# Second-layer attention: the order of scores, turns and weights between groups of steps

## The chip, the cores and the metric

The kernel runs on one core of a Trainium2 chip. The metric is the device time of one execution in microseconds (us). The kernel before took 2488.93 us in the median of three runs (2488.81 to 2493.3).

## The reference

The kernel computes a decoder of four layers on a batch of four rows of 512 tokens with 128 features, all in float32. Each layer has an attention, a cross attention and a feed-forward part. The change touches the attention of layer 2 alone (layers are counted from 0). It has 16 heads of 8 features and adds up three attentions with gates of their own per token:

```python
q = _rope(x @ Wq, HD); k = _rope(x @ Wk, HD); v = x @ Wv
sc = jnp.einsum('bhsd,bhnd->bhsn', q4, ck4) * SCALE    # 32 compressed blocks of 16 tokens
a_comp = _masked_softmax(sc, comp_mask[None, None])
ss = jnp.einsum('bhsd,bhmd->bhsm', q4, ks4) * SCALE    # 16 selected tokens
a_sel = _masked_softmax(ss, (causal_sel & valid[:, None, :])[:, None])
sw = jnp.einsum('bhsd,bhtd->bhst', q4, k4) * SCALE     # a causal window of 32 tokens
a_win = _masked_softmax(sw, wmask[None, None])
out = g[..., 0:1] * out_comp + g[..., 1:2] * out_sel + g[..., 2:3] * out_win
return out @ Wo + bo
```

A softmax over a fully masked row gives zeros.

## The kernel before

**Two lanes.** The batch is split over two lanes. Lane 0 takes rows 0 and 2, lane 1 first a short preparation and then rows 1 and 3; each stage is done for both rows of a lane before the next stage begins. A lane has its own four PSUM banks, scratch and semaphores. Both lanes share the engines. For each engine a unit gives a generator that yields between pieces. A planner (`plan`, L3051) runs all pieces with estimated costs before the kernel is built, starting at each point the piece that can begin first, and so fixes one order per engine for the whole kernel. On the chip each engine works through that order and waits on semaphores.

**Layer-2 attention** (`l2_attn`, from L1736). After a prelude (projections, rotary position, compressed keys and values, the selection of two blocks, gates) the 512 queries of a row are handled in J = 16 steps of 32 queries. For a step the 16 heads x 32 queries are four tiles of 128 rows, and each row has C = 112 keys: 64 of the window, 32 compressed, 16 selected. Four steps form a group (GR = 4, NG = 4 groups). A step j of group g passes through these stages:

- **spread** (GpSimd, L1953): the queries times the head mask into `qb`, two buffers. It waits until the scores of step j - 2 are in PSUM.
- **scores** (TensorE, L1855): four products with `kall` into bank 0 or 1, by turns. It waits for the mask of step j - 2 and for `qb`. In float32 a product is two passes, so a step shows as 8 records.
- **mask** (VectorE, L2079): scores plus mask, from PSUM into `sc`, which has two buffers of a whole group.
- **shift** (VectorE, L2029 to L2036), once for a group: the maximum of each 16 keys, of each of the three parts (three small steps L2031, three small steps L2034), and the subtraction over 128x1792.
- **exponential** (ScalarE, L1941), once for a group, over 128x1792.
- **weigh** (VectorE, L2042 to L2057), once for a group: the sums, their reciprocals times the gates, three copies into `wt7`.
- **product** (GpSimd, L1968), once for a group: exponentials times weights over 128x1792.
- **turn** (TensorE, L1864): four transposes of a step's probabilities into bank 2, which is the only one. It waits for the copy of step j - 1.
- **copy** (ScalarE, L1936): bank 2 into `pT`, two buffers.
- **values** (TensorE, L1875): four products with `vall` into bank 3. The first of a group waits until the group before has been picked.
- **pick** (VectorE, L2065 and L2069), once for a group: the own head's part of bank 3 is kept and summed into `oT`.

After the last group the output projection (L1890) and two additions (L2091, L2094) end the unit. The normalization of the lane's next unit is worked in at the end (`norm.means`, `norm.apply`, `norm.tensor`, `norm.scalar`, `norm.gpsimd`).

**Orders before.** TensorE runs a loop over i that issues turn(i - 5), scores(i), values(i - 6), so the turns of group g begin right ahead of the scores of the second step of group g + 1, and scores and turns alternate. VectorE issues mask(i), after each fourth mask the shift of that group, then the first mask of the next group, weigh, and three more masks; a pick stands after the second mask. ScalarE alternates copies and, at each fourth index, an exponential. GpSimd issues spread(i + 1) and, at each fourth i, the product of the group before.

## Time and profile before

| | |
|---|---|
| median of 3 runs | 2488.93 us (2488.81 to 2493.3) |
| the profiled execution | 2484.5 us |
| its span | 2482.7 us |
| TensorE granted clock, mean of the span | 0.824 of full speed |
| VectorE busy | 1649.3 us |
| TensorE busy | 1928.5 us |
| ScalarE busy | 1035.8 us |
| GpSimd busy | 592.6 us |

The profile comes from one execution, which has its own time beside the median. The span is what the profiler saw between the first and the last instruction. Busy times of TensorE hold waits inside its pipeline, and the ends of its products are modelled. The names of engines in the rows are PE (TensorE, with PEld for its weight loads), DVE (VectorE), ACT (ScalarE) and POOL (GpSimd); "idle before" is followed by what ended most of the idle time. The rows come from the page, from the table by stretches, from the groups by line and from the timeline, in which successive instructions of one line are merged (x3).

### The profile page before, as it was taken

How to read it: one execution, taken by the hardware profiler on the slowest of the kernel's cores; microseconds unless marked ns; L12 is line 12 of the kernel's file. 1: busy time of each engine (PE TensorE's matmuls, PEld its weight loads, DVE VectorE, ACT ScalarE, POOL GpSimd, SP SyncE). 2: the span in 40 equal slices, each digit the busy share in tenths (PEclk: the TensorE clock that was granted, in tenths of full speed). 3: DMA queues.
4: the chain of work that ended last, by engine and by line, in shares of the span. 5: the costliest groups of instructions: out<-in, count | busy, mean ns of one | idle time of the engine just before them, and what ended most of it. 6: DMA issues, size and time to landing. Idle time of an engine off the chain costs nothing. (4 is left out here: it accounts for less than half of the span.)

```text
span 2482.7 us, 31166 instructions
## 1 busy us (share of the span) xinstructions
PE 1928.5 (78%) x11373; PEld 1097.1 (44%) x11378; DVE 1649.3 (66%) x3698; ACT 1035.8 (42%) x1618; POOL 592.6 (24%) x520
## 2 busy tenths in 40 slices
PE   4788887888797777799998867669866665699972
PEld 2553544546363232367776655545532221234331
DVE  5665757575666454453637898994469988985566
ACT  1226555564644343343333223233245345425561
POOL 0003323242330010000001543530025634721000
PEclk8888998989897688799999778766667877879965
DMA  4002112030302000000000000000000000000000
GB/s 159 1 1 57 43 44 55 17 82 7 92 1 89 1 1 1 1 22 1 1 1 1 1 1 1 1 1 1 1 0 1 0 0 0 0 1 1 1 5 13
DMA packets 19224, 43.78 MB, mean 18 GB/s; under 512 B 5323, under 2 KB 7935, under 8 KB 18175
## 3 DMA queue, kind: packets, MB, share of 16 engines
q1 hardware_dynamic: 19071, 41.78, 6.0%
q8 instruction: 91, 1.49, 0.3%
q14 instruction: 62, 0.51, 0.1%
HBM read 16.59 MB, written 1.05 MB: 7 GB/s over the span
## 5 line engine op out<-in xcount | busy, mean ns | idle before, releaser
L2265 PE MATMUL lane_banks<-l_attn_lane_hc,base 128*128 128x512 f32 x256 | 176.6, 806 | 111.4 <-DVE l_attn_lane_hc L2418 111.1
L2343 POOL TENSOR_TENSOR l_attn_lane_u<-l_attn_lane_xp,l_attn_lane_bn 128x512 f32<-128x512 f32 x128 | 182.1, 1449 | 190.4 <-ACT l_attn_lane_bn L2318 190.4
L2409 DVE TENSOR_TENSOR_SCAN l_attn_lane_h<-l_attn_lane_da,l_attn_lane_u 128x512 f32<-128x512 f32 x128 | 187.7, 1501 | 5.4 <-ACT l_attn_lane_da L2326 3.2
L595 POOL TENSOR_SCALAR lane_next_rstd<-lane_next_mv 128x4 f32<-128x4 f32 x48 | 12.9, 270 | 729.0 <-DVE lane_next_mv L572 729.0
L1644 ACT ACTIVATE l_ffn_lane_hT<-lane_banks,weights 128x512 f32<-128x512 f32 x128 | 87.9, 688 | 144.5 <-PE lane_banks L1598 144.1
L1448 ACT ACTIVATE l_attn_lane_ex<-lane_banks 128x768 f32<-128x768 f32 (+3 forms) x128 | 87.0, 703 | 138.1 <-PE lane_banks L1406 137.9
L2265 PEld LDWEIGHTS lane_banks<-l_attn_lane_hc,base 128*128 128x128 f32 x256 | 58.2, 249 | 189.3 <-DVE l_attn_lane_hc L2418 146.8
L1690 DVE SCALAR_TENSOR_TENSOR l_ffn_lane_eo<-lane_banks,l_ffn_lane_sel,l_ffn_lane_eo 128x128 f32<-128x128 f32 x224 | 63.0, 344 | 97.2 <-PE lane_banks L1620 96.4
L1620 PEld LDWEIGHTS lane_banks<-weights,l_ffn_lane_hT 128*128 128x128 f32 x1024 | 119.8, 192 | 15.8 <-issue 12.2
L1620 PE MATMUL lane_banks<-weights,l_ffn_lane_hT 128*128 128x128 f32 x1024 | 122.6, 276 | 0.9 <-DVE l_ffn_lane_eo L1690 0.9
L2318 ACT ACTIVATE l_attn_lane_bn<-lane_banks 128x512 f32<-128x512 f32 x64 | 37.9, 594 | 195.9 <-PE lane_banks L2259 192.9
L1509 DVE TENSOR_REDUCE l_attn_lane_mx<-lane_banks 128x4 f32<-128x1024 f32 (+2 forms) x64 | 94.6, 1488 | 28.7 <-PE lane_banks L1387 28.6
L978 PE MATMUL lane_banks<-f_attn_lane_work,weights 128*128 128x512 f32 x128 | 81.0, 753 | 32.9 <-ACT f_attn_lane_work L1098 32.0
L1953 POOL TENSOR_TENSOR l_attn_lane_qb<-l_attn_lane_qT,base 128x512 f32<-128x512 f32 x64 | 85.4, 1344 | 88.2 <-PE lane_banks L1855 75.3
L1855 PE MATMUL lane_banks<-l_attn_lane_kall,l_attn_lane_qb 128*128 128x112 f32 x512 | 85.7, 325 | 25.3 <-DVE l_attn_lane_sc L2079 19.3
L1936 ACT ACTIVATE l_attn_lane_turns<-lane_banks 112x512 f32<-112x512 f32 x64 | 37.3, 593 | 136.5 <-PE lane_banks L1864 136.4
L1855 PEld LDWEIGHTS lane_banks<-l_attn_lane_kall,l_attn_lane_qb 128*128 128x128 f32 x512 | 79.7, 238 | 29.9 <-DVE l_attn_lane_sc L2079 22.7
L1136 POOL TENSOR_TENSOR f_attn_lane_work<-f_attn_lane_work,f_attn_lane_rden 128x512 f32<-128x512 f32 x64 | 67.1, 1051 | 104.2 <-DVE f_attn_lane_rden L1177 104.2
L2573 ACT ACTIVATE l_xattn_lane_ex<-lane_banks 77x1024 f32<-77x1024 f32 x64 | 64.9, 1020 | 63.7 <-PE lane_banks L2504 63.7
L582 DVE TENSOR_SCALAR lane_rows<-x,lane_next_mv,lane_next_rstd 128x128 f32<-128x128 f32 x192 | 66.3, 415 | 33.6 <-POOL lane_next_rstd L596 33.3
L2326 ACT ACTIVATE l_attn_lane_da<-l_attn_lane_dt,a 128x512 f32<-128x512 f32 x128 | 85.9, 714 | 2.2 <-DVE l_attn_lane_h L2409 1.8
L2418 DVE TENSOR_TENSOR l_attn_lane_hc<-l_attn_lane_h,lane_banks 128x512 f32<-128x512 f32 x128 | 80.9, 672 | 3.3 <-PE lane_banks L2267 3.1
(531 smaller groups left out, 4700.8 us busy)
## 6 DMA issues: line engine op xcount, KB each, us to landing
f_attn_lane_work<-f_attn_lane_work SPq DMA_DIRECT2D x256, 64.0 KB, 2.0
weights<-packed SPq DMA_DIRECT2D x1, 4564.5 KB, 19.8
f_attn_lane_vb<-f_attn_lane_va SPq DMA_DIRECT2D x8, 512.0 KB, 4.5
f_attn_lane_vb<-f_attn_lane_va SPq DMA_DIRECT2D x8, 384.0 KB, 5.8
weights<-packed SPq DMA_DIRECT2D x1, 2320.0 KB, 8.4
weights<-packed SPq DMA_DIRECT2D x1, 2091.0 KB, 13.6
out<-x SPq DMA_DIRECT2D x4, 256.0 KB, 2.2
weights<-packed SPq DMA_DIRECT2D x1, 897.0 KB, 9.5
```

What stands on the lines that cost most here:

```text
L978: pe.matmul(ps(2 + n % 2), w("pairones"), sq, start=True, stop=True).then_inc(*s.up("norms_in_psum"))
L1448: act.activation(ex[:, kt % 2, h:h + 2, 0:T - P * kt], banks(0, 2)[:, :, 0:T - P * kt], ACT.Exp, scale=scale)\
L1509: v.tensor_reduce(mx[:, j, t, :], banks(0, R)[:, :, 0:n], AX.X, ALU.max).then_inc(*s.up("row_max"))
L1620: last = pe.matmul(ps(2)[:, tile(t)], hT[:, n % 2, c, tile(t)], w("m1_w2", (2 * (e - 1) + c) * D, (2 * (e - 1) + c + 1) * D), start=(c == ...
L1644: act.activation(hT[:, n % 2, c, :], ps(c), ACT.Relu, bias=w("m1_b1", b, b + 1)).then_inc(*s.up("hidden_ready"))
L1855: last = pe.matmul(ps(j % 2)[:, g * C:(g + 1) * C], qb[:, j % 2, tile(g)], kall[:, j, :], start=True, stop=True)
L1953: g_.tensor_tensor(qb[:, j % 2, :].rearrange("p (h q) -> p h q", h=A2_H), bc(qT[:, 32 * j:32 * j + 32], A2_H), w("headmask").rearrange("p ...
L2265: pe.matmul(ps(2 + c), w("ident"), hc[:, c, :], start=(n == 1), stop=(n == NS)).then_inc(*s.up("state_added"))
L2326: act.activation(da[:, i % 3, :], dt[:, c, :], ACT.Exp, scale=net.a3[:, c, n:n + 1]).then_inc(*s.up("da_ready"))
L2343: g.tensor_tensor(u[:, i % 3, :], dtx[:, c, :], bn[:, n % 2, :], ALU.mult).then_inc(*s.up("u_ready"))
L2409: v.tensor_tensor_scan(h[:, c, :], da[:, i % 3, :], u[:, i % 3, :], 0.0, ALU.mult, ALU.add).then_inc(*s.up("scanned"))
L2418: v.tensor_tensor(hc[:, c, :], h[:, c, :], ps(1), ALU.mult).then_inc(*s.up("hc_ready"))
```

## The change

The order in which the four engines issue the parts of this attention is written anew. Within a group q, TensorE issues all four scores, then for the group before it turn, turn, values, turn, values, turn, values; the last values of a group come after the first scores of the group after next. VectorE issues four masks, weigh of the group before, pick of the group before that, and then the shift of the group just masked. ScalarE issues the exponential of group q between the second and third copy of group q - 1. GpSimd issues the four spreads of a group and then the product of the group before. What each part computes, its buffers and the semaphores it waits on stay as they were. The planner lays out both lanes anew from these orders.

```diff
--- before.py
+++ after.py
@@ -1876,13 +1876,19 @@
                                  start=True, stop=True)
             last.then_inc(*s.up("values_in_psum"))
 
-        for i in range(J + 6):
-            if 5 <= i < J + 5:
-                yield from turn(i - 5)
-            if i < J:
-                yield from scores(i)
-            if i >= 6:
-                yield from values(i - 6)
+
+        for q in range(NG + 1):
+            for j in range(GR * q, GR * q + GR):
+                if q < NG:
+                    yield from scores(j)
+                if q >= 2 and j == GR * q:
+                    yield from values(j - GR - 1)
+            if q >= 1:
+                for j in range(GR * (q - 1), GR * q):
+                    yield from turn(j)
+                    if j % GR:
+                        yield from values(j - 1)
+        yield from values(J - 1)
         yield from norm.tensor(pe, ps(1), norm.to_come)
         yield
         pe.wait_ge(*s.at("o_ready", NG))
@@ -1926,19 +1932,25 @@
             act.wait_ge(*s.at("vwin_in_psum", q + 1))
             act.activation(vall[0:64, GR * q:GR * q + GR, :], ps(1 + q % 2)[0:64, :].rearrange("p (j d) -> p j d", j=GR), ACT.Copy)\
                .then_inc(*s.up("vwin_ready"))
-        for i in range(J + 5):
-            if i >= 5:
-                j = i - 5
+
+        def copy_turned(j):
+            yield
+            act.wait_ge(*s.at("pT_in_psum", j + 1))
+            if j >= 2:
+                act.wait_ge(*s.at("values_in_psum", j - 1))
+            act.activation(pT[0:C, j % 2, :], ps(2)[0:C, :], ACT.Copy).then_inc(*s.up("pT_ready"))
+
+        for q in range(NG + 1):
+            if q >= 1:
+                for j in range(GR * (q - 1), GR * q - 2):
+                    yield from copy_turned(j)
+            if q < NG:
                 yield
-                act.wait_ge(*s.at("pT_in_psum", j + 1))
-                if j >= 2:
-                    act.wait_ge(*s.at("values_in_psum", j - 1))
-                act.activation(pT[0:C, j % 2, :], ps(2)[0:C, :], ACT.Copy).then_inc(*s.up("pT_ready"))
-            if i % GR == GR - 1 and i < J:
-                g = i // GR
-                yield
-                act.wait_ge(*s.at("shifted", g + 1))
-                act.activation(sc[:, g % 2, :, :, :], sc[:, g % 2, :, :, :], ACT.Exp, scale=scale).then_inc(*s.up("exp_ready"))
+                act.wait_ge(*s.at("shifted", q + 1))
+                act.activation(sc[:, q % 2, :, :, :], sc[:, q % 2, :, :, :], ACT.Exp, scale=scale).then_inc(*s.up("exp_ready"))
+            if q >= 1:
+                for j in range(GR * q - 2, GR * q):
+                    yield from copy_turned(j)
         yield from norm.scalar(act, ps(1), norm.to_come)
 
     def gpsimd(g_):
@@ -1955,14 +1967,14 @@
 
         yield
         g_.wait_ge(*s.at("q_ready", 1))
-        yield from spread(0)
-        for i in range(J + 1):
-            if i + 1 < J:
-                yield from spread(i + 1)
-            if i >= GR and i % GR == 0:
-                g = i // GR - 1
-                if i == J:
-                    yield from norm.gpsimd(g_)
+        for q in range(NG + 1):
+            for j in range(GR * q, GR * q + GR):
+                if q < NG:
+                    yield from spread(j)
+            if q == NG:
+                yield from norm.gpsimd(g_)
+            if q >= 1:
+                g = q - 1
                 yield
                 g_.wait_ge(*s.at("weights_ready", g + 1))
                 g_.tensor_tensor(sevenths(g), sevenths(g), bci(wt7[:, g % 2, :, :].rearrange("p r n -> p (r n)"), 16), ALU.mult)\
@@ -2069,25 +2081,24 @@
             v.tensor_reduce(oT[:, P * g:P * (g + 1)].rearrange("p (j q) -> p j q", j=GR),
                             r[:, g % 2, :, :].rearrange("p j (h q) -> p j q h", h=4), AX.X, ALU.add).then_inc(*s.up("o_ready"))
 
-        for i in range(J + 6):
-            if i < J:
-                g = i // GR
+        for g in range(NG):
+            for j in range(GR * g, GR * g + GR):
                 yield
-                v.wait_ge(*s.at("scores_in_psum", i + 1))
-                if g >= 2 and i % GR == 0:
+                v.wait_ge(*s.at("scores_in_psum", j + 1))
+                if g >= 2 and j == GR * g:
                     v.wait_ge(*s.at("pT_in_psum", GR * (g - 1)))
-                v.tensor_tensor(sc[:, g % 2, i % GR, :, :], ps(i % 2)[:, 0:4 * C].rearrange("p (g c) -> p g c", g=4),
-                                bc(mask[:, i, :], 4), ALU.add).then_inc(*s.up("masked"))
-                if i % GR == GR - 1:
-                    yield from shift(g)
-            if i == J:
-                yield from norm.means(v, norm.to_come)
-            if i % GR == 0 and GR <= i <= J:
-                yield from weigh(i // GR - 1)
-            if i == J:
-                yield from norm.apply(v, norm.to_come)
-            if i >= 9 and i % GR == 1:
-                yield from pick(i // GR - 2)
+                v.tensor_tensor(sc[:, g % 2, j % GR, :, :], ps(j % 2)[:, 0:4 * C].rearrange("p (g c) -> p g c", g=4),
+                                bc(mask[:, j, :], 4), ALU.add).then_inc(*s.up("masked"))
+            if g >= 1:
+                yield from weigh(g - 1)
+            if g >= 2:
+                yield from pick(g - 2)
+            yield from shift(g)
+        yield from norm.means(v, norm.to_come)
+        yield from weigh(NG - 1)
+        yield from norm.apply(v, norm.to_come)
+        yield from pick(NG - 2)
+        yield from pick(NG - 1)
         st.link(v.tensor_tensor(x, x, bc(w("a2_bo"), NT), ALU.add))
         yield
         v.wait_ge(*s.at("y_in_psum", 1))
```

## Rows read from the trace of the kernel before

**Rows 1.** The page: the span, and busy time by engine (share of the span).

```profile
span 2482.7 us, 31166 instructions
PE 1928.5 (78%) x11373; PEld 1097.1 (44%) x11378; DVE 1649.3 (66%) x3698; ACT 1035.8 (42%) x1618; POOL 592.6 (24%) x520
```

**Rows 2.** Table by stretches: us, busy PE, PEld, DVE, ACT, POOL, clock, DMA, GB/s.

```profile
1360.00:1395.00 35.00, 28.92 (x168) 22.60 (x169) 27.51 (x61) 10.69 (x19) 11.58 (x8) 0.65 0.00 0
...
1410.00:1469.00 59.00, 37.59 (x288) 29.93 (x288) 56.70 (x117) 14.94 (x20) 29.86 (x18) 0.72 0.00 1
...
1325.00:1695.00 370.00, 267.51 (x1971) 207.47 (x1972) 318.50 (x728) 111.67 (x184) 149.74 (x102) 0.76 0.00 1
```

**Rows 3.** VectorE's groups by line and shape, 1325 to 1695: busy us, mean ns | idle.

```profile
L2079 DVE TENSOR_TENSOR l_attn_lane_sc<-lane_banks,l_attn_lane_mask 128x448 f32<-128x448 f32 x64 | 38.3, 618 | 14.3 <-PE lane_banks L1855 14.0
...
L2042 DVE TENSOR_REDUCE l_attn_lane_sm<-l_attn_lane_sc 128x112 f32<-128x1792 f32 x16 | 32.2, 2015 | 2.1 <-ACT l_attn_lane_sc L1941 1.6
...
L2034 DVE TENSOR_SCALAR l_attn_lane_mx<-l_attn_lane_mx 128x64 f32<-128x64 f32 x16 | 9.7, 609 | 0.5
...
L2034 DVE TENSOR_SCALAR l_attn_lane_mx<-l_attn_lane_mx 128x32 f32<-128x32 f32 x16 | 6.2, 387 | 0.0
...
L2034 DVE TENSOR_SCALAR l_attn_lane_mx<-l_attn_lane_mx 128x16 f32<-128x16 f32 x16 | 5.0, 311 | 0.0
```

**Rows 4.** Timeline 1325 to 1370: start, us, engine, line, operation [idle before].

```profile
1325.30 1.17 PE L1790 MATMUL lane_banks<-weights,lane_xnT 128*32 128x3 f32 x32 [0.44 <-DVE x L1728]
...
1357.96 2.01 DVE L2029 TENSOR_REDUCE l_attn_lane_mx<-l_attn_lane_sc 128x112 f32<-128x1792 f32 x1
...
1360.45 0.37 DVE L2034 TENSOR_SCALAR l_attn_lane_mx<-l_attn_lane_mx 128x64 f32<-128x64 f32 x3
...
1360.86 2.02 DVE L2036 TENSOR_TENSOR l_attn_lane_sc<-l_attn_lane_sc,l_attn_lane_mx 128x1792 f32<-128x1792 f32 x1
...
1362.91 1.70 ACT L1941 ACTIVATE l_attn_lane_sc<-l_attn_lane_sc 128x1792 f32<-128x1792 f32 x1 [2.87 <-DVE l_attn_lane_sc L2036]
...
1365.25 2.01 DVE L2042 TENSOR_REDUCE l_attn_lane_sm<-l_attn_lane_sc 128x112 f32<-128x1792 f32 x1
...
1369.20 0.35 DVE L2057 COPY l_attn_lane_wt<-l_attn_lane_sm 128x64 f32<-128x64 f32 x3
...
1369.63 3.24 POOL L1968 TENSOR_TENSOR l_attn_lane_sc<-l_attn_lane_sc,l_attn_lane_wt 128x1792 f32<-128x1792 f32 x1 [11.40 <-DVE l_attn_lane_wt L2057]
```

**Rows 5.** Timeline, single steps of the loop and the end of a row.

```profile
1347.49 1.94 PE L1855 MATMUL lane_banks<-l_attn_lane_kall,l_attn_lane_qb 128*128 128x112 f32 x16
...
1353.80 1.92 PE L1855 MATMUL lane_banks<-l_attn_lane_kall,l_attn_lane_qb 128*128 128x112 f32 x8 [1.43 <-POOL l_attn_lane_qb L1953]
...
1414.38 0.66 PE L1875 MATMUL lane_banks<-l_attn_lane_turns,l_attn_lane_vall 112*32 112x128 f32 x8
...
1414.97 0.81 PE L1864 MATMUL lane_banks<-base,l_attn_lane_sc 128*112 128x128 f32 x4
...
1460.07 3.24 POOL L1968 TENSOR_TENSOR l_attn_lane_sc<-l_attn_lane_sc,l_attn_lane_wt 128x1792 f32<-128x1792 f32 x1 [2.35 <-DVE l_attn_lane_wt L2057]
...
1464.50 0.60 ACT L1936 ACTIVATE l_attn_lane_turns<-lane_banks 112x512 f32<-112x512 f32 x1 [8.70 <-PE lane_banks L1864]
...
1475.11 0.68 DVE L2065 TENSOR_TENSOR l_attn_lane_tokens<-lane_banks,weights 128x512 f32<-128x512 f32 x1
...
1475.83 1.04 DVE L2069 TENSOR_REDUCE l_attn_lane_oT<-l_attn_lane_tokens 128x128 f32<-128x512 f32 x1
...
1479.11 0.69 DVE L2094 TENSOR_TENSOR x<-x,lane_banks 128x512 f32<-128x512 f32 x1
```

**Rows 6.** Timeline, GpSimd's spreads beside a subtraction of VectorE.

```profile
1406.00 1.26 POOL L1953 TENSOR_TENSOR l_attn_lane_qb<-l_attn_lane_qT,base 128x512 f32<-128x512 f32 x1
...
1407.42 2.03 DVE L2036 TENSOR_TENSOR l_attn_lane_sc<-l_attn_lane_sc,l_attn_lane_mx 128x1792 f32<-128x1792 f32 x1
...
1407.76 2.81 POOL L1953 TENSOR_TENSOR l_attn_lane_qb<-l_attn_lane_qT,base 128x512 f32<-128x512 f32 x1 [0.49 <-PE lane_banks L1855]
```

## The prediction

> **What bounds the kernel now.** The page comes first: the span is 2482.7 us and no engine is busy all through it, VectorE 66% and TensorE 78% [rows 1]. Its own 40 slices say too little about one stage, so the next view is the table by stretches. The four second-layer attentions (two rows of the batch in each lane) lie between 1325 and 1695 us, and there VectorE is busy 318.5 of 370 us, or 86%; TensorE's 267.5 us holds waits inside its pipeline at a mean granted clock of 0.76, ScalarE and GpSimd are half idle or more [rows 2]. So this stage is bound by VectorE, but not evenly. From 1410 to 1469, with both lanes in their loops over groups, it is busy 56.7 of 59 us, which leaves 2.3 us to win. From 1360 to 1395, where one lane computes its projections and selection, it is idle 7.5 of 35 us [rows 2]. All idle time is 370 - 318.5 = 51.5 us. The groups by line show what ended it: the masks L2079 waited 14.0 us in all for scores, the sums L2042 1.6 us for the exponential [rows 3]; the rest is projections, neighbouring stages and single handshakes. The change can only shorten a lane's own chain. A microsecond saved there counts when VectorE had nothing else to do, and not otherwise.
>
> **The costs of one group, from single instructions.** Shift is 1357.96 to 1362.88 = 4.9 us; the exponential 1.7; weigh with its three copies runs 1365.25 to 1369.55, less a 0.20 us copy of the other lane in between, so 4.15; GpSimd's product with the weights 3.24, starting 0.1 after them [rows 4]. A step's scores take 1.0 us at full clock (16 passes in 1.94) and 1.9 at half (8 passes in 1.92); a step's turns 0.8; its copy on ScalarE 0.6; its values 0.66; pick 0.68 + 1.04, together 1.75 [rows 5]. A mask takes 0.62 [rows 3], a spread 1.26 [rows 6]. I give each handshake 0.1.
>
> **The chain of one lane before,** counted from weights_ready of group g-1 to that of g, with the other lane ignored. Product 3.3; turns to 4.2; scores of the group's second step, queued behind these turns on TensorE, to 5.2; then per step values, turns, scores, so the fourth step's scores end at 10.2; its mask 10.9; shift 15.8; exponential 17.6 (the first mask of group g+1 hides under it); weigh 21.8. The first weights come 10.9 us after the last mask of group 0 (4.9 + 1.8 + 4.15). An attention's four groups take 10.9 + 3 x 21.8 = 76.3 us.
>
> **The chain after.** No instruction is added or removed: 64 spreads, masks, score, turn and value steps, 16 shifts, exponentials, products and picks remain, and no DMA is touched. Only orders move. On TensorE all four scores of a group stand ahead of the turns of the group before; on GpSimd the third and fourth spread of a group (1.26 us each) now pass the product of the group before, which costs nothing since both are done while VectorE still masks and weighs; on VectorE four masks stand ahead of weigh, and pick and shift follow it; on ScalarE the exponential of group q stands between the second and third copy of group q-1.
> - Group 0: shift 4.9, two masks that are ready, two at the pace of the scores to 8.35, weigh to 12.5. That is 1.6 us later than before; the exponential is hidden completely.
> - Middle groups, from weights_ready: product 3.3, turns 4.2, copy, turns 5.8, copy 6.5, turns 7.4. Meanwhile VectorE does pick and shift to 6.7, the exponential ends 8.45, and the third copy, queued behind it, ends 9.05 instead of 8.1. Turns 9.95, values 10.6, scores of the next group's first step 11.6, and with values, a spread and scores between them the fourth mask ends 16.5; weigh 20.7. Without a pick (the first such group) the exponential is early enough: 19.7.
> - The last group has no masks to come: pick, shift, exponential, weigh, 12.6.
> Sum 12.5 + 19.7 + 20.7 + 12.6 = 65.5 us, which is **10.8 us less chain per attention**. What follows the last weights (product, turns, values, picks, output) keeps its order and costs nothing new.
>
> **What of it reaches the end.** Four attentions give 43.2 us of chain. First way: a saved microsecond counts in the 14% of the stage in which VectorE idles, 43.2 x 0.14 = 6.0. Second way: an attention alone would last 22 (1325.3 to 1347.5, ahead of the first scores [rows 4, 5]) + 5 (four masks) + 76.3 + 20 (1460 to 1479.8, last weights to the row's end [rows 5]) = 123 us, of which 79.6 is VectorE's work (318.5 / 4) and 43.4 waiting; 10.8 is 25% of the waiting, and 25% of 51.5 us idle is 12.9. I take the middle, -9.5, and keep 3 (the masks' and sums' 15.6 us lowered by a fifth) and 13 as ends.
> Against it stands the port that VectorE and GpSimd share. The three small steps L2034 of a shift last 0.37 us together when GpSimd is still [rows 4], but over 16 groups they sum to 9.7 + 6.2 + 5.0 = 20.9 us, 15 too many, 0.9 per group [rows 3]. After the change a shift of groups 1 to 3 begins at most 1.75 us behind weights_ready, so these steps come 2.5 to 4.2 us behind it, while the product (to 3.3) or the two spreads queued behind it (to 5.8) run. I put 1.2 to 1.7 us on each of 12, which is 14 to 20 us against 15: between -1 and +5, and I take +3. The reverse is seen too: a spread beside L2036 lasted 2.81 us, not 1.26 [rows 6]. The Trainium skill says the same (GPSIMD Engine Reference, Key points): GpSimd shares its SBUF interfaces with VectorE and contends with instructions in a two-port mode or with two SBUF inputs. By that rule all 12 shifts would collide, and the sum would stand at the +5 end.
> **Sum: -9.5 + 3 = -6.5 us.** The profiled execution took 2484.5 us (2482.7 span and 1.8 around it), 4.4 under the median 2488.93 of the three runs shown; it would become 2478, and the median 2482.4. No number of this stage depends on which is used.
>
> **The rivals.**
> - *Nothing measurable.* VectorE is full in the middle (56.7 of 59) and the idle time near projections belongs to steps that the change leaves alone; the port takes the +5 and the idle gives 3: +2 us, 2491. For it: rows 2. Against it: the stretch where one lane alone feeds VectorE is just where a chain counts.
> - *Slower: the score phase outgrows its cover.* From the end of a shift to the fourth mask of the next group a lane now offers VectorE only 2.5 us of work; all else waits on exponential, copy, turns, values and scores. That is 16.5 - 6.7 = 9.8 us at full clock. At the half clock (a step's scores 1.9 us) it is 1.8 + 0.6 + 1.1 + 0.7 + 1.9 to the first scores, 6.4 for three more at that pace and a mask of 0.65: 13.2. The other lane's weigh, pick and shift are 10.8 us, and with the lane's own 2.5 the cover is 13.3. It decides once the phase is longer; one spread held up by 1.5 us makes it 14.7, and 1.4 us of idle in each of the 12 groups is 17, less the 6.5: 10 us slower, 2499. For it: the granted clock is 0.65 from 1360 to 1395 [rows 2]. Also queued behind the moved exponential are two copies and, behind these, all scores of the next group, so a shift that the other lane's work holds up stops TensorE for both. Against it: a pair of groups, one of each lane, holds 2 x 13.3 = 26.6 us of VectorE's work, and the new chain of 20.7 leaves 5.9 of slack under it, the old one of 21.8 only 4.8.
> - *The gain is not the size of the sum.* The order of the two lanes on every engine is fixed by a planner from estimated costs, so all later stages are laid out anew, too. I can only bound it by the spread of the runs and the gaps of one handover, about 5 us either way; I put it into the range.
>
> **How the numbers follow.** A measurement of this kernel can tell about 0.2%, 5 us, from no change. The forecast, 2482.4, has 0.52 (its own range 2471 to 2488); nothing measurable 0.28; slower by the score phase or a bad layout 0.20. Part of the forecast's range lies within 5 us of before, and part of the second rival below it, which I let cancel. Faster 0.50, same 0.29, slower 0.21. The low end is 2488.9 - 12.9 - 5 = 2471, the high end 2496, short of the slower rival's 2499.
>
> **What would show it.** Right: first masks of a group following each other ahead of weigh, no wait of L2042 for L1941, each lane's four groups shorter by some 10 us where the other lane is in its projections, and VectorE's idle time in the stage down from 51.5 to about 42. Wrong: L2034 rising well over 20.9 us in all; L2079 waiting over 14 us for scores; or the stage shorter but the stages behind it longer.

## The result, and the profile after

The kernel after took 2510.21 us in the median of four runs (2507.84 to 2518.06), against 2490.15 for the kernel before on the same chip. The ratio is 1.0091 (95% interval 1.0063 to 1.0119): slower by 20 us, four times what such a measurement can tell from no change. The forecast was 2482.4 with a range to 2496, so both sign and range were wrong. The profiled execution of after is the slowest of its four, 2518.06 against 2484.5, and all sums below are between these two single executions. The one of after lies 8 us above its median and that of before 6 below, and in which stages is not known.

The page of the kernel after, as [rows 1]:

```profile
span 2516.3 us, 31163 instructions
PE 1959.3 (78%) x11378; PEld 1101.3 (44%) x11378; DVE 1658.5 (66%) x3698; ACT 1034.5 (41%) x1616; POOL 581.0 (23%) x520
```

Shares and counts are nearly as before, so the page alone tells little. The units' ends tell where the time went. Up to 1325 us both traces agree within 0.7 us. From there I call "the stage" what lies between the end of lane 0's last first-layer feed-forward part and the end of lane 1's last attention of layer 2: **364.0 us before, 395.3 after, +31.3.** From there to the last addition of the program are 779.7 and 781.3 us. So the loss arises in the stage that the change edits. VectorE is busy 316.0 us of it before and 326.1 after, **idle 48.0 and 69.2**: +21.2 of idle and +10.1 of busy time.

Table by stretches of after (columns as in [rows 2]), and behind it one stretch of before:

```profile
1360.00:1395.00 35.00, 21.63 (x133) 15.98 (x133) 29.15 (x61) 11.26 (x17) 8.41 (x7) 0.60 0.00 1
1395.00:1470.00 75.00, 46.36 (x352) 37.09 (x350) 62.44 (x131) 16.08 (x21) 31.25 (x22) 0.75 0.00 1
...
1325.00:1727.00 402.00, 280.18 (x1970) 209.61 (x1968) 331.93 (x737) 112.47 (x184) 145.25 (x102) 0.74 0.00 1
```

```profile
1395.00:1470.00 75.00, 47.07 (x357) 38.46 (x355) 70.47 (x143) 18.03 (x24) 41.91 (x25) 0.73 0.00 1
```

Where one lane is alone, VectorE is busier than it was (29.15 of 35 us, [rows 2]: 27.51). But in the middle, from 1395 to 1470, it idled 4.5 us before and idles 12.6 now. So 8.0 of the 21.2 us of new idle time arose where the prediction had seen VectorE full.

VectorE's groups of after, 1325 to 1727, as [rows 3]:

```profile
L2090 DVE TENSOR_TENSOR l_attn_lane_sc<-lane_banks,l_attn_lane_mask 128x448 f32<-128x448 f32 x64 | 39.0, 618 | 30.4 <-PE lane_banks L1855 30.1
L2048 DVE TENSOR_TENSOR l_attn_lane_sc<-l_attn_lane_sc,l_attn_lane_mx 128x1792 f32<-128x1792 f32 x16 | 34.4, 2150 | 0.6
...
L2054 DVE TENSOR_REDUCE l_attn_lane_sm<-l_attn_lane_sc 128x112 f32<-128x1792 f32 x16 | 32.2, 2010 | 0.8 <-ACT l_attn_lane_sc L1950 0.7
L582 DVE TENSOR_SCALAR lane_rows<-x,lane_next_mv,lane_next_rstd 128x128 f32<-128x128 f32 x32 | 25.1, 845 | 2.2 <-POOL lane_next_rstd L596 2.2
...
L2046 DVE TENSOR_SCALAR l_attn_lane_mx<-l_attn_lane_mx 128x16 f32<-128x16 f32 x16 | 8.3, 518 | 0.0
L2046 DVE TENSOR_SCALAR l_attn_lane_mx<-l_attn_lane_mx 128x64 f32<-128x64 f32 x16 | 7.3, 459 | 0.5
...
L2046 DVE TENSOR_SCALAR l_attn_lane_mx<-l_attn_lane_mx 128x32 f32<-128x32 f32 x16 | 6.2, 387 | 0.0
```

The masks' work is the same (618 ns each), but **their wait for scores rose from 14.0 to 30.1 us**. The three small steps, L2034 before and L2046 now, sum to 21.8 us against 20.9: the collision that I had priced there did not grow. Most of the rest of the busy time is on the subtraction (34.4 against 32.4), the copies of weights (10.7 against 8.7) and the normalization L582 (28 of them in the stage, count times mean: 25.7 against 21.0), 8.7 us together; other pieces became up to 2.7 us longer or shorter.

The waits of the stage, first those of before, then of after (engine, line and what it waited for: us in all, times, longest):

```profile
PE lane_banks L1864 <- POOL l_attn_lane_sc L1968: 23.8, 9, 5.2
...
PE lane_banks L1855 <- DVE l_attn_lane_sc L2079: 19.3, 7, 3.9
...
PE lane_banks L1864 <- ACT l_attn_lane_turns L1936: 2.5, 9, 0.6
```

```profile
DVE l_attn_lane_sc L2090 <- PE lane_banks L1855: 30.1, 28, 3.0
PE lane_banks L1864 <- POOL l_attn_lane_sc L1980: 30.0, 7, 9.4
...
PE lane_banks L1864 <- ACT l_attn_lane_turns L1941: 25.9, 28, 6.0
PE lane_banks L1855 <- DVE l_attn_lane_sc L2090: 25.7, 8, 7.2
```

TensorE's turns waited 2.5 us for copies before and wait 25.9 now, and its scores wait 25.7 us for masks while the masks wait 30.1 us for scores. That is no shortage of an engine: two engines that work in a fixed order wait for each other in turn. In the timeline of after it looks so; an exponential of ScalarE, then VectorE, then TensorE:

```profile
1386.63 1.70 ACT L1950 ACTIVATE l_attn_lane_sc<-l_attn_lane_sc 128x1792 f32<-128x1792 f32 x1 [0.92 <-DVE l_attn_lane_sc L2048]
```

```profile
1398.64 0.62 DVE L2090 TENSOR_TENSOR l_attn_lane_sc<-lane_banks,l_attn_lane_mask 128x448 f32<-128x448 f32 x1 [3.04 <-PE lane_banks L1855]
1402.05 0.62 DVE L2090 TENSOR_TENSOR l_attn_lane_sc<-lane_banks,l_attn_lane_mask 128x448 f32<-128x448 f32 x1 [2.79 <-PE lane_banks L1855]
...
1405.27 2.01 DVE L2054 TENSOR_REDUCE l_attn_lane_sm<-l_attn_lane_sc 128x112 f32<-128x1792 f32 x1
...
1409.33 0.62 DVE L2090 TENSOR_TENSOR l_attn_lane_sc<-lane_banks,l_attn_lane_mask 128x448 f32<-128x448 f32 x1
...
1416.07 3.63 DVE L2046 TENSOR_SCALAR l_attn_lane_mx<-l_attn_lane_mx 128x64 f32<-128x64 f32 x3
...
1424.57 2.03 DVE L2048 TENSOR_TENSOR l_attn_lane_sc<-l_attn_lane_sc,l_attn_lane_mx 128x1792 f32<-128x1792 f32 x1
1426.51 1.15 DVE L2090 TENSOR_TENSOR l_attn_lane_sc<-lane_banks,l_attn_lane_mask 128x448 f32<-128x448 f32 x2
```

```profile
1410.01 3.75 PE L1855 MATMUL lane_banks<-l_attn_lane_kall,l_attn_lane_qb 128*128 128x112 f32 x16 [3.53 <-DVE l_attn_lane_sc L2090]
...
1427.18 3.76 PE L1855 MATMUL lane_banks<-l_attn_lane_kall,l_attn_lane_qb 128*128 128x112 f32 x16 [7.21 <-DVE l_attn_lane_sc L2090]
...
1472.92 1.10 PE L1864 MATMUL lane_banks<-base,l_attn_lane_sc 128*112 128x128 f32 x4 [9.36 <-POOL l_attn_lane_sc L1980]
```

The lanes can be told apart by their semaphores. Up to 1405 VectorE idles between masks of lane 0, while lane 0's weigh behind them (L2054 at 1405.27) stands still; its exponential had ended at 1388.3, 17 us earlier. Then weigh runs, lane 1's mask comes only at 1409.33, and TensorE has stood 3.53 us for it. The 7.21 us of TensorE at 1427 are another case: VectorE was busy for 7.1 us of it, with the end of lane 1's shift and the whole of lane 0's, and lane 1's masks come behind both at 1426.51. Just before, the three small steps of lane 1's shift had taken 3.63 us.

The first case is the common one. I measured it over the whole stage: **during 26.4 of the 30.1 us in which VectorE waited for scores, the weigh of the same lane was ready** (its exponential had ended) and stood behind the mask; in before it was 0 of 14.0. The other lane's weigh was ready in 3.3 us of them. A weigh began 10.1 us after the end of its exponential on average, 0.3 before.

### The profile page after: what moved, and what is told of

It is laid out like the page before. It is cut to its first block and busy times, and to the rows that moved or that the text cites. A ratio compares the mean times of both kernels' runs of the same rounds, so it can differ in the third digit from the quotient of the medians.

```text
span 2516.3 us, 31163 instructions
## 1 busy us (share of the span) xinstructions
PE 1959.3 (78%) x11378; PEld 1101.3 (44%) x11378; DVE 1658.5 (66%) x3698; ACT 1034.5 (41%) x1616; POOL 581.0 (23%) x520
## 5 line engine op out<-in xcount | busy, mean ns | idle before, releaser
L2276 PE MATMUL lane_banks<-l_attn_lane_hc,base 128*128 128x512 f32 x256 | 181.7, 827 | 99.8 <-DVE l_attn_lane_hc L2429 99.7
L2354 POOL TENSOR_TENSOR l_attn_lane_u<-l_attn_lane_xp,l_attn_lane_bn 128x512 f32<-128x512 f32 x128 | 176.8, 1408 | 210.4 <-ACT l_attn_lane_bn L2329 210.3
L1855 PE MATMUL lane_banks<-l_attn_lane_kall,l_attn_lane_qb 128*128 128x112 f32 x512 | 85.7, 331 | 29.8 <-DVE l_attn_lane_sc L2090 25.7
L1864 PE MATMUL lane_banks<-base,l_attn_lane_sc 128*112 128x128 f32 x256 | 56.4, 363 | 56.9 <-POOL l_attn_lane_sc L1980 30.0
L1855 PEld LDWEIGHTS lane_banks<-l_attn_lane_kall,l_attn_lane_qb 128*128 128x128 f32 x512 | 78.5, 239 | 38.5 <-DVE l_attn_lane_sc L2090 28.6
L582 DVE TENSOR_SCALAR lane_rows<-x,lane_next_mv,lane_next_rstd 128x128 f32<-128x128 f32 x192 | 70.9, 438 | 35.6 <-POOL lane_next_rstd L596 35.4
```

The costliest lines, as they stand in the source:

```text
L582: v.tensor_scalar(m.xn[:, t, :], m.x[:, t, :], ln.next_mv[:, t, 0:1], ln.next_rstd[:, t:t + 1], ALU.subtract, ALU.mult).then_inc(m.normed, 1)
L1855: last = pe.matmul(ps(j % 2)[:, g * C:(g + 1) * C], qb[:, j % 2, tile(g)], kall[:, j, :], start=True, stop=True)
L2276: pe.matmul(ps(2 + c), w("ident"), hc[:, c, :], start=(n == 1), stop=(n == NS)).then_inc(*s.up("state_added"))
L2354: g.tensor_tensor(u[:, i % 3, :], dtx[:, c, :], bn[:, n % 2, :], ALU.mult).then_inc(*s.up("u_ready"))
```

## The experiments

In the ratios each kernel is compared with the kernel before on its own chip (medians there 2484.7 to 2487.9 us). "Stage" and "idle" are measured in each profiled execution as above.

### One lane alone: are the two chains what I counted?

Lane 1 leaves out layers 2 and 3; the same edit was made to before and to after.

```diff
-                units += [(seg, f, args, row) for seg, f, args in parts]
+                if i == 0 or parts[0][0][:2] in ("l0", "l1"):
+                    units += [(seg, f, args, row) for seg, f, args in parts]
```

> The kernel before, with rows 1 and 3 (lane 1) leaving out layers 2 and 3, so that lane 0 has the engines to itself from the second-layer attention on. It measures the chain of one lane alone. Theory A (the chain sums of the prediction are right and the loss comes from the two lanes together): from the end of the fourth mask of group 0 to the third copy of the last weights 76 us, within 4; one period between the products of successive groups 21.8. Theory B (the sums are wrong): something else, and the lane-alone kernels then show which step was mis-sized.

> The changed kernel, cut in the same way. Theory A: 65.5 us for the same stretch, within 4, about 11 less than the same stretch of the kernel before cut so, and middle periods of 20.7; the change is then a gain for a lane alone. Theory B: no shorter than before, or longer; the exponential ahead of two copies, or scores that wait for four turns in a row, then shows as idle time of TensorE ahead of L1864 or L1855.

Measured: lane 0's two attentions last 128.0 + 121.8 = 249.8 us before and 126.9 + 117.2 = 244.2 after. That is 1.1 and 4.6 us less, 2.8 on average, not 10.8. The stretch named in the expectations, from the fourth mask of group 0 to the third copy of the last weights, took 78.5 and 77.3 us before (expected: 76 within 4) and 77.4 and 74.3 after (expected: 65.5 within 4). So the sum of before held and that of after did not. From first to fourth product of a row are 65.6 and 66.4 us before (predicted 3 x 21.8 = 65.4) and 59.8 and 59.6 after (predicted 53.0). The periods before are 21.1 to 22.8 us, as counted. After they are 23.3, 23.7, 12.8 in one row and 22.6, 24.2, 12.8 in the other: the last, without masks, as counted (12.6), the middle ones 2.6 to 3.6 us too long (19.7 and 20.7). The timeline of after alone, second period:

```profile
1397.41 3.24 POOL L1980 TENSOR_TENSOR l_attn_lane_sc<-l_attn_lane_sc,l_attn_lane_wt 128x1792 f32<-128x1792 f32 x1 [6.11 <-DVE l_attn_lane_wt L2069]
...
1400.71 1.10 PE L1864 MATMUL lane_banks<-base,l_attn_lane_sc 128*112 128x128 f32 x4 [8.15 <-POOL l_attn_lane_sc L1980]
...
1401.39 1.83 DVE L2046 TENSOR_SCALAR l_attn_lane_mx<-l_attn_lane_mx 128x64 f32<-128x64 f32 x3
...
1402.59 1.08 PE L1864 MATMUL lane_banks<-base,l_attn_lane_sc 128*112 128x128 f32 x4 [0.78 <-ACT l_attn_lane_turns L1941]
...
1407.64 1.07 PE L1864 MATMUL lane_banks<-base,l_attn_lane_sc 128*112 128x128 f32 x4 [1.53 <-ACT l_attn_lane_turns L1941]
...
1409.23 2.05 PE L1855 MATMUL lane_banks<-l_attn_lane_kall,l_attn_lane_qb 128*128 128x112 f32 x8
...
1411.32 0.62 DVE L2090 TENSOR_TENSOR l_attn_lane_sc<-lane_banks,l_attn_lane_mask 128x448 f32<-128x448 f32 x1 [6.04 <-PE lane_banks L1855]
```

And before alone:

```profile
1390.97 1.88 PE L1855 MATMUL lane_banks<-l_attn_lane_kall,l_attn_lane_qb 128*128 128x112 f32 x8
...
1396.43 0.65 PE L1864 MATMUL lane_banks<-base,l_attn_lane_sc 128*112 128x128 f32 x4
...
1396.91 1.04 PE L1855 MATMUL lane_banks<-l_attn_lane_kall,l_attn_lane_qb 128*128 128x112 f32 x8
```

Both orders leave TensorE still while the weights are made (12.78 us before, 8.15 after), and both find it at the half clock (mean granted clock 0.50 for the first 5.9 us before and the first 8.5 us after): turns 1.10 and not 0.65, a step's scores 1.88 or 2.05 and not 1.04. Before, TensorE then has turns and scores by turns, without a gap, and the third scores after the restart take 1.04 again, at a granted clock of 1.00. After, it has only turns, each held by the copy of the turn before (0.78 us idle in the row at 1402.59), and the fourth by a copy that stood behind the exponential (1.53). So it is still at the half clock for the first scores, 8.5 us later. I had priced turns at 0.8 and scores at 1.0 throughout. The row behind the 0.8 (1414.97 in [rows 5]) lies across a change of level, at a mean granted clock of 0.76, while the 0.66 for the values comes from a stretch at 0.50; at the full clock they take 0.43 (lane alone). The small steps L2046 take 1.83 us beside GpSimd's two spreads, against the 0.37 that my chain had (the +3 for the port was added outside the chain). Counted from the weights in this period, the exponential ends 1.2 us later than in my chain, the fourth turns 1.4, the first scores 2.4 and the fourth mask 3.1. Over both attentions the small steps sum to 4.4 us before and 11.6 after, the subtractions to 16.2 and 18.2, and VectorE's whole busy time rises from 1205.7 to 1215.5 us.

A lane's own attentions do gain, then, by 5.6 us in these two executions. The whole kernels took the same time, 2147.22 and 2147.55 us, one execution each: the stage of after began 3.7 us later, and what follows it took 2.2 us longer, both in code that nobody had edited. A loss of 20 us appears only with both lanes.

### Whose order is it? ScalarE's and VectorE's, one at a time

exp_last puts the exponential behind all four copies; dve_old gives VectorE its order of before (one mask of the next group, weigh, three more masks) and keeps the other three engines as after.

```diff
 # exp_last, ScalarE
-                for j in range(GR * (q - 1), GR * q - 2):
+                for j in range(GR * (q - 1), GR * q):
                     yield from copy_turned(j)
...
-                for j in range(GR * q - 2, GR * q):
-                    yield from copy_turned(j)
```

> The changed kernel with one part of it taken out: ScalarE issues the exponential of a group behind all four copies of the group before, not between the second and the third. Theory 1 (the exponential, which waits for the shift, holds up two copies, so turns and scores): TensorE's idle time ahead of L1864 that a copy ended falls from 25.9 us to under 10, the masks' wait for scores from 30.1 to about 20, and the time from 2510 to some 2498. Theory 2 (VectorE's four masks in a row stand at the pace of the scores): 2508 to 2512, masks' wait unchanged near 30. Theory 3 (the planner's new layout, in which the two lanes fall into step): any time between 2490 and 2520, unrelated to the wait that was taken out.

Measured: 2508.85 us, ratio 1.0097 (1.0075 to 1.0119), stage 388.4 with 62.8 idle. Its waits:

```profile
DVE l_attn_lane_sc L2087 <- PE lane_banks L1855: 29.7, 29, 3.7
...
PE lane_banks L1864 <- ACT l_attn_lane_turns L1941: 24.1, 33, 5.4
```

This is what theory 2 had said: the time and the masks' wait stay. But the turns' wait for copies, which the edit was to take out, is still 24.1 us and not under 10, so it does not come from the exponential's place alone. The stage of this execution is 6.9 us shorter, the time is not: the exponential between the copies is not what costs the 20 us.

> The changed kernel with VectorE's order as it was before (shift right behind its fourth mask, then one mask, weigh, three masks), the other three engines as changed. Theory 1: no gain, 2508 to 2515, since the exponential still stands ahead of two copies. Theory 2: back to 2490 to 2498, the masks' wait back to under 20 us. Theory 3: any time between 2490 and 2520.

Measured: **2471.99 us, ratio 0.9942 (0.992 to 0.9963)**, stage 360.1 with 47.2 idle. That is below every range that I had given. With VectorE's order undone, the other three orders are 13 us faster than before (2484.7 on that chip), where all four are 20 slower. Its waits:

```profile
PE lane_banks L1855 <- DVE l_attn_lane_sc L2091: 38.0, 11, 6.0
...
PE lane_banks L1864 <- ACT l_attn_lane_turns L1941: 25.4, 28, 4.9
...
DVE l_attn_lane_sc L2091 <- PE lane_banks L1855: 9.0, 10, 1.5
```

The masks' wait is down to 9.0 us, yet TensorE's wait for copies is still 25.4. So that wait is no loss by itself (about half of it, 13.2 us, comes with TensorE's and GpSimd's orders alone, in pe_pool below), and TensorE's scores wait even longer for masks than in after (38.0 against 25.7). What costs, in this layout, is VectorE standing at masks: 21.1 of the 22.0 us of idle time between this run and after.

### A series: two and three masks ahead of weigh, and the shift before it

```diff
                                 bc(mask[:, j, :], 4), ALU.add).then_inc(*s.up("masked"))
-            if g >= 1:
-                yield from weigh(g - 1)
-            if g >= 2:
-                yield from pick(g - 2)
+                if g >= 1 and j % GR == 1:        # 2 for masks3
+                    yield from weigh(g - 1)
+                if g >= 2 and j % GR == 2:        # 3 for masks3
+                    yield from pick(g - 2)
             yield from shift(g)
```

> The changed kernel with two masks of a group ahead of weigh of the group before (pick behind the third mask), where the changed kernel has four and the kernel before has one. The run with one took 2472 beside 2509 for four. Theory 2 (each further mask in front of weigh holds the last weights back for the time in which the next scores come, and with them product, turns and copies): the time rises step by step with the number, about 12 us for each: 2484 here; TensorE's wait for the product L1980 lies between 0 (one mask) and 30 us (four). Theory 3 (layout luck of the planner): no order in the series, and this one may lie anywhere from 2470 to 2515.

> The same with three masks ahead of weigh. Theory 2: 2496, between two and four masks, TensorE's wait for the product between 10 and 30 us. Theory 3: anywhere from 2470 to 2515, out of order.

In shift_first all four masks come first, then the shift, and weigh and pick behind it.

> The changed kernel with a group's shift right behind its four masks and ahead of weigh and pick of the groups before: the weights come later still, by one shift of 4.9 us. Theory 2 (late weights cost): slower than 2509, by 5 to 20 us, with a longer wait of TensorE for the product than 30 us. Theory 2b (what costs is only the idle time of VectorE at the four masks, and the shift belongs right behind them): at or below 2509, the masks' wait still near 30 us.

| masks ahead of weigh | time, us | ratio (95%) | stage | idle | masks' wait |
|---|---|---|---|---|---|
| 1 (dve_old) | 2471.99 | 0.9942 (0.992–0.9963) | 360.1 | 47.2 | 9.0 |
| 2 (masks2) | 2478.12 | 0.9973 (0.9959–0.9988) | 357.9 | 42.6 | 7.1 |
| 3 (masks3) | 2495.16 | 1.0033 (1.0016–1.005) | 375.0 | 57.5 | 17.0 |
| 4 (after) | 2510.21 | 1.0091 (1.0063–1.0119) | 395.3 | 69.2 | 30.1 |
| 4 and the shift (shift_first) | 2524.12 | 1.0153 (1.0136–1.017) | 408.1 | 95.6 | 58.8 |

The later the weights, the slower. Expected were 2484, 2496 and 5 to 20 us above after; 2478, 2495 and 14 above came. The stage is longer only from three masks on. The time in which VectorE waits for scores while the same lane's weigh stands ready goes the same way: 2.0, 4.2, 13.2, 26.4 and 28.5 us. The waits of shift_first:

```profile
POOL l_attn_lane_sc L1980 <- DVE l_attn_lane_wt L2069: 102.2, 13, 21.6
...
DVE l_attn_lane_sc L2090 <- PE lane_banks L1855: 58.8, 36, 7.4
...
PE lane_banks L1864 <- POOL l_attn_lane_sc L1980: 53.4, 6, 17.2
```

One could read here that late weights make GpSimd's product late (102.2 us of waiting against 68.3 in after), that the turns stand for the product (53.4 against 30.0), and that the next scores are queued behind these turns. That chain is argued and not shown. TensorE's wait for the product does grow along the series (1.1, 20.5, 22.7, 30.0 and 53.4 us), but GpSimd's wait for weights does not (51.7, 76.8, 53.9, 68.3 and 102.2), and the fastest kernel of all, before_hop below, has 56.6 us of the first. Still, "four masks ahead of weigh is the fault" looked settled at this point.

### Another layout: is it the order or the interleaving?

The planner lays the two lanes into one order per engine by estimated costs. Its estimates can be changed without touching the kernel's work: the delay between engines from 0.15 to 0.3 us, or TensorE's costs by 1.5. Both were done to before and to after, with no other edit.

```diff
-HOP = 0.15
+HOP = 0.3
```

> The kernel before with the planner's cost of a handshake at 0.3 us in place of 0.15: the same programs, interleaved anew on every engine. It shows how far a new layout alone moves the kernel. Theory 2: the attention stage stays within 10 us of its 364 us, and stays shorter than the changed kernel's laid out with the same costs. Theory 3: the stage moves by 20 us or more, as far as the change moved it.

> The changed kernel with the same handshake cost of 0.3 us in the planner. Theory 2: its attention stage stays 20 us or more longer than that of the kernel before with this cost. Theory 3: the two stages lie within 10 us of each other, in either order.

> One mask ahead of weigh, the other three engines as changed, laid out with a handshake of 0.3 us in the planner. With that cost the kernel before took 2457 and the changed one 2472, stages 347 and 358 us. Theory 2 (the order of VectorE alone makes the loss, in any layout): stage 340 to 348 us and 2450 to 2457. Theory 3: a stage above 352 us, the gain of one mask not repeated.

> Two masks ahead of weigh with a handshake of 0.3 us in the planner. Theory 2: a stage between those of one and four masks in this layout, 345 to 355 us, 2453 to 2465. Theory 3: out of order, outside 340 to 360 us.

```diff
-        return self.work(0.05 + share * width(out) * (0.0006 if rhs.dtype == BF16 else 0.0018))
+        return self.work(0.05 + share * width(out) * (0.0006 if rhs.dtype == BF16 else 0.0027))
...
-        return self.work(0.06 + 0.0009 * width(out))
+        return self.work(0.06 + 0.0014 * width(out))
```

> The kernel before, laid out with TensorE's costs half higher in the planner (a third layout). If the changed orders cost time in any layout: the changed kernel so laid out has a stage at least 10 us longer than this one. If the loss is the layout's: the two lie within 5 us, or the changed one is shorter.

> The changed kernel in the third layout. Orders themselves: stage 10 us or more above that of before_pe. Layout: within 5 us of it or shorter; then the loss of the change is what the planner makes of it with costs that leave the half clock out.

| layout | before: time, ratio, stage busy + idle | after: the same | after less before: stage, busy, idle |
|---|---|---|---|
| as given | 2490.15, –, 316.0 + 48.0 | 2510.21, 1.0091, 326.1 + 69.2 | +31.3, +10.1, +21.2 |
| delay 0.3 | **2457.02, 0.9885 (0.986–0.9911)**, 304.2 + 42.9 | 2472.31, 0.9946 (0.993–0.9963), 308.7 + 49.2 | +10.8, +4.5, +6.3 |
| TensorE x 1.5 | 2506.61, 1.0081 (1.0064–1.0098), 309.5 + 71.5 | 2497.23, 1.004 (1.0024–1.0056), 314.7 + 59.0 | -7.3, +5.2, -12.5 |

Against before as given on its own chip, the layout alone moves the kernel before by -28 and +20 us, and it turns the sign of the change: +20, +15, -9 us. By the marks set beforehand, the stage of before moved by 17 us, between the two theories, and the stages of the two kernels differ by 10.8 in the second layout, just outside the 10 of theory 3; in the third the mark for the layout is met. Where before itself is laid out badly, its masks wait as much as those of after did. The masks of before with TensorE's costs raised, then of after with the same costs:

```profile
PE lane_banks L1864 <- POOL l_attn_lane_sc L1968: 46.5, 9, 15.5
...
DVE l_attn_lane_sc L2079 <- PE lane_banks L1855: 32.9, 25, 4.0
```

```profile
PE lane_banks L1864 <- POOL l_attn_lane_sc L1980: 31.0, 11, 6.9
...
DVE l_attn_lane_sc L2090 <- PE lane_banks L1855: 23.6, 18, 2.1
```

What does hold in all three layouts is that weigh stands ready behind masks after the change and not before it: in 26.4, 21.4 and 15.2 us of the masks' wait after, in 0 before. But before with TensorE's costs raised idles 71.5 us, as much as after as given, without any of it. So this is one source of idle time among others, and it does not decide the sign.

And the series does not repeat. With the delay at 0.3, one mask ahead of weigh takes 2471.49 us (ratio 0.9944, 0.9928 to 0.9961; stage 358.4), two 2463.22 (0.9911, 0.9894 to 0.9927; 350.1), four 2472.31 (357.9): one and four are equal. So VectorE's order explains the loss in the layout as given, and is no rule. The busy term is above zero in all three layouts. The stage can't be compared for it in the third layout, where that of after holds 24 of the L582 and that of before 28; the whole kernel can, with the same 3698 instructions on VectorE: 1649.3 and 1658.5 us, 1655.3 and 1657.5, 1654.7 and 1670.1. That is +9.2, +2.2 and +15.4. These are single executions, and a new layout without any edit to VectorE's order moves the same sum by as much (before: 1649.3 to 1655.3; pe_pool below: 1656.3), so the +2.2 says nothing.

### The parts that seem good, and the normalization

pe_pool is before with TensorE's and GpSimd's orders of after alone; pe_pool_hop is that with the delay 0.3.

> The kernel before with the changed orders of TensorE and GpSimd alone; VectorE (one mask ahead of weigh) and ScalarE (exponential between third and fourth copy) as before. Beside the run with one mask, 2472, it differs by ScalarE's order alone. If the gain there came from TensorE's order (a group's scores not behind turns that wait for the product): 2468 to 2478, with TensorE waiting under 3 us for the product. If ScalarE's order made it: 2482 to 2490. If it was the planner's layout: anywhere from 2455 to 2500.

> The changed orders of TensorE and GpSimd alone, with a handshake of 0.3 us in the planner. In the first layout they gained 8 us beside the kernel before. If the gain is theirs: stage 340 to 345 us and 2448 to 2455, faster than the 2457 of the kernel before in this layout. If it was the layout's: 2457 to 2475, as the run with one mask ahead of weigh, which differs by ScalarE's order alone.

Measured: 2479.56 us, ratio 0.997 (0.996 to 0.998), stage 351.0; and 2458.54, 0.9886 (0.9869 to 0.9902), stage 343.8. Against before in the same layout these two orders shorten the stage by 13.0 and 3.3 us, and the masks' wait is 7.6 us in the first. But what follows the stage, whose code is the same, took 788.8 us in pe_pool against 779.7 in before, and 768.4 against 765.1: 9.1 of the 13.0 and all of the 3.3 were lost where nothing had been edited (and in pe_pool the stage also began 4.9 us earlier). Both runs missed the range for a gain that is TensorE's order's own (2468 to 2478, and 2448 to 2455), the first narrowly; TensorE's wait for the product, expected under 3 us, was 4.5 in it. dve_old differs from pe_pool by ScalarE's order alone, the exponential one copy earlier; its stage is 9.1 us longer (360.1 against 351.0), and with the delay 0.3 it is 14.6 longer (358.4 against 343.8). In the first layout the whole kernel is none the slower for it (ratio 0.9942 against 0.997). In the second it is 13 us slower (2471.49 against 2458.54), and VectorE's order adds nothing to that (2472.31): **there the loss of 15 us comes with ScalarE's order, in the layout as given with VectorE's.**

apply_late moves the normalization L582 behind the last two picks, in after:

```diff
         yield from weigh(NG - 1)
-        yield from norm.apply(v, norm.to_come)
         yield from pick(NG - 2)
         yield from pick(NG - 1)
+        yield from norm.apply(v, norm.to_come)
```

> The changed kernel with the normalization of the lane's next unit (four steps L582, which lasted 8.9 us beside two products of GpSimd) behind the last two picks instead of behind the last weigh. If the shared port is a main part of the loss: L582 and its kin shorter by 5 us or more, time 2495 to 2503. If not: 2505 to 2515, whatever L582 does.

Measured: 2503.15 us, ratio 1.0061 (1.0044 to 1.0077). L582 fell from 25.7 to 10.5 us and VectorE's busy time from 326.1 to 319.3, but idle rose from 69.2 to 76.5, and the stage stayed at 395.8. That collision was taken away, but the three small steps rose from 21.8 to 27.8 us, so part of it only moved. The stage did not become shorter: what was no longer busy became idle. The time fits neither mark (2495 to 2503, 2505 to 2515), by a hair above the first. In the profiled executions the gain lies in later stages (763.8 against 781.3 us), laid out anew. The collision itself, in after, VectorE and GpSimd:

```profile
1469.67 8.90 DVE L582 TENSOR_SCALAR lane_rows<-x,lane_next_mv,lane_next_rstd 128x128 f32<-128x128 f32 x4
```

```profile
1469.58 6.49 POOL L1980 TENSOR_TENSOR l_attn_lane_sc<-l_attn_lane_sc,l_attn_lane_wt 128x1792 f32<-128x1792 f32 x2 [7.07 <-DVE l_attn_lane_wt L2069]
1476.03 2.46 POOL L1965 TENSOR_TENSOR l_attn_lane_qb<-l_attn_lane_qT,base 128x512 f32<-128x512 f32 x2
```

## Why the prediction was wrong

- **The chain before** was right: 21.8 us counted for a period, 21.1 to 22.8 measured with a lane alone.
- **The chain after** was mis-sized. The first weights, which I had put 1.6 us later, came 4.7 and 3.8 us later, counted from the fourth mask in the two rows (the first product starts 9.0 and 9.2 us behind the start of its exponential, 6.0 before). "Middle groups" took 22.6 to 24.2 us instead of 19.7 and 20.7, by the half clock that follows TensorE's idle time, by the copy behind the exponential and by the small steps beside the spreads. The last group was right (12.8 for 12.6). The "10.8 us less chain per attention" is 1.1 and 3.0 over the same stretch in a lane alone. So by this estimate four attentions had about 8 us of chain to give, not 43.2.
- **The step that failed is "What of it reaches the end".** I turned chain into idle time by a share (14%, or 25% of the waiting) and got -9.5. The idle time changed by +21.2, +6.3 and -12.5 us in three layouts, and the forecast sign appeared only in the third. A share assumes that the two lanes slide freely past each other. Here the planner has fixed each engine's order: a late mask stands in front of its own lane's ready weigh (26.4 of the 30.1 us), and that weigh then in front of the other lane's mask. I had named 56.7 busy of 59 us as a bound on what could be won in the middle, and had not asked what could be lost there: 8.0 us.
- **The port** was put at +3, between -1 and +5. Over the whole kernel it is +9.2, +2.2 and +15.4 by layout, and +9.8 for a lane alone with only two attentions: a right sign for a lane alone, and too small a size; with two lanes a new layout moves the same sum by 6 us without the change, so the +2.2 at least is no evidence. For a lane alone the place was right, the three small steps (+7.2) and the subtraction (+2.0). In after as given the small steps rose by 0.9 only, and most of the rest lies at the subtraction, the copies and L582, which I had not looked at; with TensorE's costs raised they went from 12.9 to 26.5 us. Which of VectorE's pieces stands beside a product is a matter of the layout, and a chain of one lane can't show it. The Trainium skill (GPSIMD Engine Reference, Key points), cited in the prediction, says that GpSimd contends with VectorE's instructions in a two-port mode or with two SBUF inputs. By that, the reductions, with one input, and the masks, with one of two inputs in PSUM, should not suffer, and the traces agree: no reduction over 128x1792 took more than 2.02 us and no mask more than 0.63, before or after.
- **The rival "the score phase outgrows its cover"** described in the main what the layout as given shows, VectorE idle between the masks of a group: I gave it 17 us of idle time, and the idle rose by 21.2, of which the masks' wait is 16.1. It also named that queued turns stop both lanes, and the half clock. Its "against", 5.9 us of slack under a pair of groups, again assumed free sliding. It got 0.20. It is no rule of this change: in the second layout the loss of 15 us does not come with the four masks, and in the third the sign turns. Of the signs named beforehand, the masks' wait above 14 us came (30.1), the small steps well above 20.9 did not (21.8), and the weighs' wait for exponentials fell to 0.7 us, as the forecast had it, while the idle time went up instead of down to 42.
- **The rival "the gain is not the size of the sum"** got 5 us either way. Two changes of the planner's estimates moved the same kernel by -28 and +20 us. The range to 2496 was too short for that.
- **The median and the sum:** in the profiled executions, idle +21.2, busy +10.1, later stages +1.6 and the start +0.7 give the 33.6 us between 2484.5 and 2518.06; the medians differ by 20, since the profiled execution of after was 8 us above its median and that of before 6 us below.

What stays open: which pair of pieces in the two other layouts makes the idle time smaller or larger. The waits show where it is, not why the planner's order meets it. Nor is it known why the series climbs with the masks in the first layout and not in the second, and why the loss comes with VectorE's order in one and with ScalarE's in the other.

Of all that was run, the fastest is the kernel before with the planner's delay at 0.3, **2457.02 us (0.9885)**, equal to pe_pool_hop (2458.54). It is faster than before and after as given, and it does not contain the change.

## What to carry to other kernels

Where two streams share engines in an order fixed beforehand, what the chain of one stream gains says little. Measure the change in two or three layouts (a changed estimate of the planner is enough) before you credit or blame it, and put the spread of these layouts into the range. Look for pieces that stand ready behind pieces still to come on an in-order engine: here, a weigh behind four masks and not one cost some 37 us in one layout (ratios 1.0091 and 0.9942) and nothing in another (0.9946 and 0.9944), so it is a place to try and no rule. And price a chain's TensorE steps at the clock that its own idle time leaves them.

## What the runs showed of the hardware

- Four L582 over 128x128, 0.38 us each in the mean of apply_late (10.5 us for 28), took 8.90 us in a row beside two products and two spreads of GpSimd, which kept their 3.24 and 1.25 us each. Here VectorE bore it all; beside a subtraction GpSimd's spread did ([rows 6], 2.81 for 1.26).
- After 8.15 us of idle TensorE, turns took 1.10 us and the first scores, 8.5 us later with only turns, values and gaps between, still 2.05, at a granted clock of 0.50. With scores among the turns, after 12.78 us of idle, they were back at 1.04 and a granted clock of 1.00 6.8 us after the restart. These are the two levels, 1.2 and 2.4 GHz.
- An estimate in the planner raised from 0.15 to 0.3 us, with the same instructions, made the kernel before 1.15% faster; what follows the stage went from 779.7 to 765.1 us.
